# Linear attention of layer 1: from four passes of eight batches to one stream over eight groups of four batches

## The chip, the cores and the metric

The kernel runs on one core of one Trainium2 chip. Its engines work side by side: TensorE (matrix products, PE in the profile, its weight loads PEld), VectorE (DVE), ScalarE (ACT), GpSimd (POOL) and SyncE (SP, which here only issues transfers). Products land in PSUM, eight banks of 128 x 512 f32; everything else lives in SBUF. The metric is the device time of one execution in microseconds (us), the median of several.

## The reference, cut to what matters

The whole program is a decoder of four layers over x of 32 batches x 128 tokens x 128 channels. The change is in one sublayer, the attention of layer 1, followed by a residual sum and a layer norm:

```python
phi = lambda x: jax.nn.elu(x) + 1.0              # max(x, 0) + exp(min(x, 0))
q = phi(heads(x @ Wq.T + bq))                    # 16 heads of 8 channels
k = phi(heads(x @ Wk.T + bk))
v = heads(x @ Wv.T + bv)
kv = jnp.einsum('bhtd,bhtm->bhdm', k, v)
z = 1.0 / (jnp.einsum('bhtd,bhd->bht', q, k.sum(axis=2) + EPS) + EPS)
out = jnp.einsum('bhtd,bhdm,bht->bhtm', q, kv, z)
x = _layernorm(x + out.reshape(...) @ Wo.T + bo)
```

There is no mask in this sublayer, so each batch has one 128 x 128 summary k.T v, cut to the 16 diagonal blocks of 8 x 8 that belong to heads.

## The kernel before, in words

`decoder` runs the sublayers one after another. Each is a block of its own: every engine has its list of instructions, semaphores order them, and at the end of a block (`sublayer`, L31) all engines meet. `l1_attn` is called through `chunks("b", ...)` (L3092), which runs it four times, each time on eight batches (`NB = 8`, two groups of `GB = 4`) with buffers `r_b` and `xt_b`.

One pass, on eight batches:
- TensorE transposes the eight batches of x into two banks (L59), ScalarE copies them to `xt_b` (L1400). TensorE makes Q transposed for both groups (L1351, one product of 512 columns a group). Then, per group, K (L1356) with its bias as a second product of a row of ones with the bias row (L1358, weights of one row), four times, and V (L1356) four times.
- The feature map is elu + 1. VectorE takes from each bank the part below zero (L1427) and the part above (L1428), for Q with the bias as a per-partition number; ScalarE takes the exponential of the former (L1403), GpSimd adds the two (L1420). VectorE adds V's bias (L1432).
- Then a loop over the eight batches, one batch at a time, in three steps skewed by one batch each: summary (L1367, K features against V with a column of ones behind it, so that column 128 is the sum of K), mask (L1439, L1440, L1442), read-out (L1374, 144 columns: 128 of the result and 16 denominators), normalise (L1447, L1449, L1453), transpose (L1383), copy (L1407), output projection (L1386), residual (L1466).
- GpSimd has put x + bo into `r_b` beforehand (L1416). The layer norm takes statistics on VectorE (L68, L72), the root on ScalarE (L107), its reciprocal and the scaling on VectorE (L80, L83).

ScalarE needs one function table for the exponential and one for the root, and loads them in each pass (L102, L1403). f32 products are two records each in the trace, a high and a low half; transpositions are one record. The order of the work is the order in which the code is written; there is no planner.

Of the kernel before, what the change touches and what calls it, by code (L numbers as in the profile page):

```python
# [15 lines left out]
B_ALL = 32  # L16
# [1317 lines left out]
def l1_attn(nc, E):  # L1334
# [3 lines left out]
    with sublayer(nc, "xt_ps xt qk_ps v_ps neg pos ex q v kv_ps kvm ks kvd n_ps den rz zn zt_ps zt o_ps rb res" + LN) as (s, ctx):  # L1338
        sb = E.scratch(ctx)
        NEGP = sb("NEG", [P, 2 * NG, GT]); Q = sb("Q", [P, 2 * NG, GT])  # L1340
        V = sb("V", [P, NB, P + 1])
        KVD = sb("KVD", [P, 2, P + H]); KS = sb("KS", [P, NB]); DEN = sb("DEN", [P, 2, H]); RZ = sb("RZ", [P, 2, H])
        ZN = sb("ZN", [P, 2, P]); ZT = sb("ZT", [P, 2, P]); R = E.r
        with nc.Block() as block:
            @block.tensor
            def _(pe):
                for g in range(NG):
                    pe_transpose4(nc, [E.x[:, g * GB + b, :] for b in range(GB)], PS[:, g, :], E.ident).then_inc(s.xt_ps, 1)
                for g in range(NG):
                    pe.wait_ge(s.xt, g + 1)  # L1350
                    nc.tensor.matmul(PS[:, 2 + g, :], W.wq, E.xt[:, g * GT:(g + 1) * GT], start=True, stop=True).then_inc(s.qk_ps, 1)  # L1351
                for g in range(NG):
                    for w, b0, bank, sem in ((W.wk, W.bk, 4 + g, s.qk_ps), (W.wv, None, 6 + g, s.v_ps)):
                        for b in range(GB):
                            o = PS[:, bank, b * P:(b + 1) * P]
                            ins = nc.tensor.matmul(o, E.xt[:, (g * GB + b) * P:(g * GB + b + 1) * P], w, start=True, stop=b0 is None)  # L1356
                            if b0 is not None:
                                ins = nc.tensor.matmul(o, E.ones_row[0:1, :], b0, start=False, stop=True)  # L1358
                        ins.then_inc(sem, 1)

                def summary(t):
                    if t % GB == 0:
                        pe.wait_ge(s.q, NG + t // GB + 1)
                        pe.wait_ge(s.v, t // GB + 1)
                    if t >= 2:
                        pe.wait_ge(s.ks, t - 1)
                    nc.tensor.matmul(PS[:, t % 2, 0:P + 1], Q[:, NG + t // GB, (t % GB) * P:(t % GB + 1) * P], V[:, t, :],  # L1367
                                     start=True, stop=True).then_inc(s.kv_ps, 1)

                def read_out(t):  # L1370
                    pe.wait_ge(s.kvd, t + 1)
                    if t >= 2:
                        pe.wait_ge(s.zn, t - 1)
                    nc.tensor.matmul(PS[:, 2 + t % 2, 0:P + H], Q[:, t // GB, (t % GB) * P:(t % GB + 1) * P], KVD[:, t % 2, :],  # L1374
                                     start=True, stop=True).then_inc(s.n_ps, 1)

                def project(t):
                    pe.wait_ge(s.zn, t + 1)
                    if t >= 2:
                        pe.wait_ge(s.res, t - 1)  # L1380
                    else:
                        pe.wait_ge(s.q, 2 * NG)
                    nc.tensor.transpose(PS[:, 4 + t % 2, 0:P], ZN[:, t % 2, :], E.ident).then_inc(s.zt_ps, 1)  # L1383
                    pe.wait_ge(s.zt, t + 1)
                    o = PS[:, 4 + t % 2, P:2 * P]
                    nc.tensor.matmul(o, ZT[:, t % 2, :], W.wo, start=True, stop=True).then_inc(s.o_ps, 1)  # L1386

                for t in range(NB + 2):
                    if t < NB:
                        summary(t)  # L1390
                    if 1 <= t <= NB:
                        read_out(t - 1)
                    if t >= 2:
                        project(t - 2)

            @block.scalar
            def _(act):
                for g in range(NG):
                    act.wait_ge(s.xt_ps, g + 1)
                    nc.scalar.copy(E.xt[:, g * GT:(g + 1) * GT], PS[:, g, :]).then_inc(s.xt, 1)  # L1400
                for c in range(2 * NG):
                    act.wait_ge(s.neg, c + 1)
                    nc.scalar.activation(NEGP[:, c, :], NEGP[:, c, :], ACT.Exp).then_inc(s.ex, 1)  # L1403
                act_table(nc, E, ACT.Sqrt)
                for t in range(NB):
                    act.wait_ge(s.zt_ps, t + 1)
                    nc.scalar.copy(ZT[:, t % 2, :], PS[:, 4 + t % 2, 0:P]).then_inc(s.zt, 1)  # L1407
                    if t == GB:
                        act_layernorm(nc, act, E, s, 0)
                act_layernorm(nc, act, E, s, 1)  # L1410

            @block.gpsimd
            def _(pool):
                nc.gpsimd.memset(V[:, :, P:P + 1], 1.0)

                nc.gpsimd.tensor_tensor(R[:], E.x[:], bc(W.bo.unsqueeze(1), [P, NB, P]), ALU.add).then_inc(s.rb, 1)  # L1416
                for c in range(2 * NG):
                    pool.wait_ge(s.ex, c + 1)
                    pool.wait_ge(s.pos, c + 1)
                    nc.gpsimd.tensor_tensor(Q[:, c, :], Q[:, c, :], NEGP[:, c, :], ALU.add).then_inc(s.q, 1)  # L1420

            @block.vector
            def _(dve):
                for c in range(2 * NG):
                    dve.wait_ge(s.qk_ps, c + 1)
                    b = W.bq if c < NG else 0.0
                    nc.vector.tensor_scalar(NEGP[:, c, :], PS[:, 2 + c, :], b, 0.0, ALU.add, ALU.min).then_inc(s.neg, 1)  # L1427
                    nc.vector.tensor_scalar(Q[:, c, :], PS[:, 2 + c, :], b, 0.0, ALU.add, ALU.max).then_inc(s.pos, 1)  # L1428

                for g in range(NG):  # L1430
                    dve.wait_ge(s.v_ps, g + 1)
                    nc.vector.tensor_tensor(V[:, g * GB:(g + 1) * GB, 0:P], PS[:, 6 + g, :].rearrange("p (b d) -> p b d", b=GB),  # L1432
                                            bc(W.bv.unsqueeze(1), [P, GB, P]), ALU.add).then_inc(s.v, 1)

                def mask_summary(t):
                    dve.wait_ge(s.kv_ps, t + 1)
                    if t >= 2:
                        dve.wait_ge(s.n_ps, t - 1)
                    nc.vector.tensor_tensor(KVD[:, t % 2, 0:P], PS[:, t % 2, 0:P], E.blockmask, ALU.mult)  # L1439
                    nc.vector.tensor_scalar(KS[:, t:t + 1], PS[:, t % 2, P:P + 1], 1e-6, None, ALU.add).then_inc(s.ks, 1)  # L1440
                    dve.wait_ge(s.ks, t + 1)
                    nc.vector.tensor_scalar(KVD[:, t % 2, P:P + H], E.headmask, KS[:, t:t + 1], None, ALU.mult).then_inc(s.kvd, 1)  # L1442

                def normalise(t):
                    dve.wait_ge(s.n_ps, t + 1)
                    n = PS[:, 2 + t % 2, :]
                    nc.vector.tensor_scalar(DEN[:, t % 2, :], n[:, P:P + H], 1e-6, None, ALU.add).then_inc(s.den, 1)  # L1447
                    dve.wait_ge(s.den, t + 1)
                    nc.vector.reciprocal(RZ[:, t % 2, :], DEN[:, t % 2, :]).then_inc(s.rz, 1)  # L1449
                    dve.wait_ge(s.rz, t + 1)  # L1450
                    if t >= 2:
                        dve.wait_ge(s.zt_ps, t - 1)
                    nc.vector.tensor_tensor(ZN[:, t % 2, :].rearrange("p (h d) -> p h d", d=D), n[:, 0:P].rearrange("p (h d) -> p h d", d=D),  # L1453
                                            bc(RZ[:, t % 2, :].unsqueeze(2), [P, H, D]), ALU.mult).then_inc(s.zn, 1)

                for t in range(NB + 2):
                    if t < NB:
                        mask_summary(t)
                    if 1 <= t <= NB:
                        normalise(t - 1)  # L1460
                    if t >= 2:
                        u = t - 2
                        dve.wait_ge(s.o_ps, u + 1)
                        if u == 0:
                            dve.wait_ge(s.rb, 1)
                        nc.vector.tensor_tensor(R[:, u, :], PS[:, 4 + u % 2, P:2 * P], R[:, u, :], ALU.add).then_inc(s.res, 1)  # L1466
                    if t == GB + 1:
                        dve.wait_ge(s.res, GB)
                        dve_ln_stats(nc, dve, E, s, 0, grp(R, 0))
# [1757 lines left out]
```

## Time and profile before

| | us |
|---|---|
| median of 3 runs | 4504.68 (4503.95 to 4505.66) |
| the profiled execution, its own time | 4501.69 |
| span of the profiled execution | 4499.9 |
| TensorE busy | 3835.1 (85%) |
| VectorE busy | 2671.2 (59%) |
| ScalarE busy | 2146.1 (48%) |
| GpSimd busy | 1089.5 (24%) |

Busy shares are means over many stages with different limits; what is worth reading is the stage at hand, from 1474.56 us to 1635.62 us of the span. Times of the trace are given from the start of the span. A busy TensorE is not a TensorE at full speed: its clock is granted at 1.2 or 2.4 GHz, and the profile gives the granted share of full speed as PEclk (0.50 or 1.00 at any moment, a mean over a stretch).

### The profile page before, as it was taken

What the parts mean: (1) busy time and instruction counts of PE and PEld (TensorE: products, weight loads), DVE (VectorE), ACT (ScalarE), POOL (GpSimd) and SP (SyncE); (2) the same over time, 40 slices, a digit from 0 to 9 for tenths busy, and PEclk for the clock granted to TensorE, in tenths of its full rate; (3) what the DMA queues carried; (4) which work ended last, traced back from release to release, by engine and by line L of the source; (5) the groups of instructions that cost most, each with busy time, mean ns of one, the idle gap of its engine ahead of it and who ended that gap; (6) DMA issues with size and microseconds to landing.
All of it is one profiled execution on the core that took longest, in us unless ns stands there. A gap on an engine that the chain in (4) does not pass through costs nothing. (4 is left out here: it accounts for less than half of the span.)

```text
span 4499.9 us, 84989 instructions
## 1 busy us (share of the span) xinstructions
PE 3835.1 (85%) x33634; PEld 2573.7 (57%) x33634; DVE 2671.2 (59%) x7185; ACT 2146.1 (48%) x3795; POOL 1089.5 (24%) x754
## 2 busy tenths in 40 slices
PE   2888888787999789898999996555679998698999
PEld 2666666565666556664555553434457776465665
DVE  6677777565888557666656555982332222476555
ACT  2666666444555235555555444530554443454332
POOL 4444434222222211004454542221200000110000
PEclk8999999998999669999999997776789999798999
DMA  4222222000000010000000000004200000000000
GB/s 120 45 48 49 49 48 47 4 1 1 1 1 1 1 53 2 1 1 1 2 2 2 2 2 1 22 22 145 87 1 1 1 1 1 29 2 2 1 10 10
DMA packets 60472, 92.10 MB, mean 20 GB/s; under 512 B 16827, under 2 KB 43662, under 8 KB 58830
## 3 DMA queue, kind: packets, MB, share of 16 engines
q1 hardware_dynamic: 55948, 80.96, 7.7%
q8 instruction: 268, 4.39, 0.4%
q10 hardware_dynamic: 4130, 5.72, 0.4%
q14 instruction: 126, 1.03, 0.1%
HBM read 42.46 MB, written 10.62 MB: 12 GB/s over the span
## 5 line engine op out<-in xcount | busy, mean ns | idle before, releaser
L854 PE MATMUL banks<-XT,weight_region 128*128 128x512 f32 x1696 | 781.7, 599 | 1.4 <-DVE T L1229 1.4
L876 PEld LDWEIGHTS banks<-weight_region,HT 128*128 128x128 f32 x4672 | 560.8, 192 | 129.3 <-issue 107.4
L876 PE MATMUL banks<-weight_region,HT 128*128 128x128 f32 x4672 | 566.1, 275 | 7.1 <-ACT HT L1011 6.5
L1252 DVE SCALAR_TENSOR_TENSOR x_res<-banks,WT,x_res 128x128 f32<-128x128 f32 x800 | 225.0, 344 | 476.4 <-PE banks L876 437.4
L854 PEld LDWEIGHTS banks<-XT,weight_region 128*128 128x128 f32 x1696 | 305.8, 193 | 288.1 <-issue 285.3
L1006 ACT ACTIVATE HT<-banks,weight_region 128x512 f32<-128x512 f32 x256 | 173.3, 687 | 240.2 <-PE banks L854 234.0
L1069 POOL TENSOR_TENSOR FNM<-FNM,FRS 128x8 f32<-128x8 f32 x16 | 3.2, 202 | 1008.3 <-ACT FRS L965 1008.3
L458 DVE TENSOR_REDUCE MX<-banks 128x8 f32<-128x1152 f32 x128 | 173.2, 1353 | 116.6 <-PE banks L275 114.8
L384 ACT COPY PT<-banks 128x384 f32<-128x384 f32 x384 | 171.6, 481 | 134.1 <-PE banks L285 132.4
L1643 ACT COPY PT<-banks 77x512 f32<-77x512 f32 x256 | 143.0, 582 | 184.4 <-PE banks L1565 184.4
L1022 ACT ACTIVATE T<-banks 128x512 f32<-128x512 f32 x128 | 76.1, 597 | 233.9 <-PE banks L854 226.0
L285 PE MATMUL banks<-sb_c_ident,SM 128*128 128x128 f32 x1152 | 179.0, 283 | 4.6 <-ACT PT L384 2.7
L427 POOL TENSOR_TENSOR KT<-KT,FL 128x512 f32<-128x512 f32 x64 | 81.5, 1273 | 374.0 <-DVE FL L447 374.0
L258 PE MATMUL banks<-XT,weight_region 128*128 128x256 f32 x512 | 145.5, 414 | 28.4 <-ACT PT L384 24.6
L399 ACT ACTIVATE SM<-SM 128x1152 f32<-128x1152 f32 x128 | 150.3, 1174 | 29.6 <-DVE SM L466 29.6
L1565 PE MATMUL banks<-sb_c_ident,SM 128*77 128x128 f32 x1024 | 160.3, 291 | 0.0
L369 ACT ACTIVATE RAW<-banks,weight_region 128x256 f32<-128x256 f32 x256 | 107.3, 471 | 108.4 <-PE banks L258 99.6
L285 PEld LDWEIGHTS banks<-sb_c_ident,SM 128*128 128x128 f32 x1152 | 128.5, 141 | 47.2 <-ACT RAW L369 13.1
L466 DVE TENSOR_TENSOR SM<-banks,MX 128x1024 f32<-128x1024 f32 x128 | 155.3, 1213 | 0.0
L1081 POOL TENSOR_TENSOR x_res<-x_res,T 128x512 f32<-128x512 f32 x64 | 85.5, 1336 | 263.8 <-ACT T L983 263.8
L1214 DVE TENSOR_TENSOR HT<-banks,T 128x512 f32<-128x512 f32 x128 | 87.8, 690 | 100.6 <-PE banks L854 92.8
L1565 PEld LDWEIGHTS banks<-sb_c_ident,SM 128*77 128x77 f32 x1024 | 114.8, 151 | 53.2 <-issue 31.6
(488 smaller groups left out, 8529.7 us busy)
## 6 DMA issues: line engine op xcount, KB each, us to landing
FL<-RAW SPq DMA_DIRECT2D x512, 64.0 KB, 2.3
T<-s4d_k_dram SPq DMA_DIRECT2D x8, 1024.0 KB, 5.8
weight_region<-in_l_ffn__w_dram SPq DMA_DIRECT2D x2, 2048.0 KB, 7.6
film_dram<-F SPq DMA_DIRECT2D x8, 512.0 KB, 2.9
weight_region<-in_l_ffn__w_dram ACTq DMA_DIRECT2D x2, 2048.0 KB
FO<-film_dram SPq DMA_DIRECT2D x8, 512.0 KB, 4.1
x_res<-in_x_dram SPq DMA_DIRECT2D x1, 2048.0 KB
weight_region<-in_l_ffn__w_dram SPq DMA_DIRECT2D x2, 1024.0 KB, 9.7
```

What stands on the lines that cost most here:

```text
L258: ins = nc.tensor.matmul(bank[:, jj * PTOK:(jj + 1) * PTOK], w[:, j * P:(j + 1) * P], XT[:, p % 2, :], start=True, stop=True)
L285: ins = nc.tensor.transpose(ring(item, n)[:, q * P:(q + 1) * P], SM[:, n % 3, 3 * c + q, :], E.ident)
L384: nc.scalar.copy(PT[:, n % 2, 3 * c:3 * c + 3, :].rearrange("p h q -> p (h q)"), ring(f"T{c}", n)[:, 0:3 * P]).then_inc(s.pt, 1)
L399: nc.scalar.activation(SM[:, n % 3], SM[:, n % 3], ACT.Exp, scale=SCALE).then_inc(s.ex, 1)
L458: nc.vector.tensor_reduce(MX[:, n % 2], sc, AXX, ALU.max).then_inc(s.mx, 1)
L466: nc.vector.tensor_tensor(SM[:, n % 3, 1:9, :].rearrange("p (a i) k -> p i a k", a=2), sc[:, :, :, 0:P], bc(MX[:, n % 2].unsqueeze(3), [P, ...
L854: nc.tensor.matmul(PS[:, q % 4, :], w, xt, start=True, stop=True).then_inc(s.h_ps, 1)
L876: ins = nc.tensor.matmul(PS[:, 4 + u % 2, b * P:(b + 1) * P], HT[:, u % 2, j, b * P:(b + 1) * P], w2[j], start=j == 0, stop=j == len(w2) - 1)
L1006: ins = nc.scalar.activation(HT[:, u % 2, j, :], PS[:, (first[u] + j) % 4, :], ACT.Gelu, bias=W.b1[:, e, j:j + 1]).then_inc(s.act_done, 1)
L1252: ins = nc.vector.scalar_tensor_tensor(R[:, t, :], PS[:, 4 + u % 2, b * P:(b + 1) * P], WT[:, t, e:e + 1], R[:, t, :], ALU.mult, ALU.add)
L1565: ins = nc.tensor.transpose(bank_of("T", k)[0:L, c * P:(c + 1) * P], SM[:, t % 3, 4 * c + a, :], E.ident)
L1643: nc.scalar.copy(PT[:, t % 2, a].rearrange("p c q -> p (c q)"), bank_of("T", k)[0:L, :]).then_inc(s.pt, 1)
```

## The change

`l1_attn` is called once, on all 32 batches, as a loop over eight groups of four batches, software-pipelined: in step i TensorE turns group i+1, makes the summary of group i, turns back the result of group i-1, makes Q, K and V of group i+1, the output of group i-1 and the read-out of group i. Buffers of a group are two deep. The other parts:
- Work that was one batch to an instruction (mask, denominators, reciprocal, normalisation, copy of ZT, residual) now takes four batches, or two where a PSUM bank holds two (masks and ZN).
- Features: ScalarE takes relu(-x) from the bank (L1446, L1450 of the new code) and then exp(-that) (L1452, L1454); VectorE makes max(x, 0) + that in one instruction (L1468, L1472). GpSimd has no part in it.
- Biases of Q and of the output are made by products too, as K's was: Q's with the bias row as weights and ones as 512 columns (L1364), the output's with a row of ones as weights, per batch (L1400).
- The residual is added in x itself (L1510), without `r_b`. The layer norm's root and reciprocal are Ln and Exp on ScalarE (`act_rstd`), in the table that is loaded at the start.

```diff
-    with sublayer(nc, "xt_ps xt qk_ps v_ps neg pos ex q v kv_ps kvm ks kvd n_ps den rz zn zt_ps zt o_ps rb res" + LN) as (s, ctx):
+    NG = B_ALL // GB
...
+        XT = sb("XT", [P, 2, GT]); EQ = sb("EQ", [P, 2, GT]); EK = sb("EK", [P, 2, GT]); QF = sb("QF", [P, 2, GT]); KF = sb("KF", [P, 2, GT])
+        bank_xt, bank_q, bank_k, bank_v = PS[:, 0, :], PS[:, 1, :], PS[:, 2, :], PS[:, 3, :]
+        bank_o = PS[:, 5, :]
+        kv = PS[:, 4:6, 0:2 * KW].rearrange("p a (b k) -> p a b k", b=2)
+        nd = PS[:, 6:8, 0:2 * NW].rearrange("p a (b k) -> p a b k", b=2)
...
+                def project_in(g):
+                    x = XT[:, g % 2, :]
                     pe.wait_ge(s.xt, g + 1)
+                    if g:
+                        pe.wait_ge(s.qf, g)
+                    nc.tensor.matmul(bank_q, W.wq, x, start=True, stop=False)
+                    nc.tensor.matmul(bank_q, W.bq, bc(E.ones_row.unsqueeze(1), [1, GB, P]), start=False, stop=True).then_inc(s.q_ps, 1)
+                    if g:
+                        pe.wait_ge(s.kf, g)
+                    for b in range(GB):
+                        o = bank_k[:, b * P:(b + 1) * P]
+                        nc.tensor.matmul(o, x[:, b * P:(b + 1) * P], W.wk, start=True, stop=False)
+                        ins = nc.tensor.matmul(o, E.ones_row, W.bk, start=False, stop=True)
+                    ins.then_inc(s.k_ps, 1)
...
+                def turn_back(g):
+                    pe.wait_ge(s.zn, g + 1)
+                    pe.wait_ge(s.xt, min(g + 3, NG))
+                    pe_transpose4(nc, [ZN[:, g % 2, b, :] for b in range(GB)], bank_xt, E.ident).then_inc(s.zt_ps, 1)
+
+                def project_out(g):
+                    pe.wait_ge(s.zt, g + 1)
+                    pe.wait_ge(s.kvd, min(g + 2, NG))
+                    for b in range(GB):
+                        o = bank_o[:, b * P:(b + 1) * P]
+                        nc.tensor.matmul(o, ZT[:, g % 2, b, :], W.wo, start=True, stop=False)
+                        ins = nc.tensor.matmul(o, E.ones_row, W.bo[0:1, :], start=False, stop=True)
+                    ins.then_inc(s.o_ps, 1)
...
+                for i in range(-1, NG + 1):
+                    if i + 1 < NG:
+                        turn(i + 1)
+                    if 0 <= i < NG:
+                        summary(i)
+                    if 1 <= i:
+                        turn_back(i - 1)
+                    if i + 1 < NG:
+                        project_in(i + 1)
+                    if 1 <= i:
+                        project_out(i - 1)
+                    if 0 <= i < NG:
+                        read_out(i)
...
+                        nc.scalar.activation(EQ[:, g % 2, :], bank_q, ACT.Relu, scale=-1.0).then_inc(s.mq, 1)
...
+                        nc.scalar.activation(EQ[:, g % 2, :], EQ[:, g % 2, :], ACT.Exp, scale=-1.0).then_inc(s.eq, 1)
...
+                    if 2 <= i:
+                        act_rstd(nc, act, E, s, i - 2)
...
+                def features(g):
+                    dve.wait_ge(s.eq, g + 1)
+                    if g >= 2:
+                        dve.wait_ge(s.n_ps, g - 1)
+                    nc.vector.scalar_tensor_tensor(QF[:, g % 2, :], bank_q, 0.0, EQ[:, g % 2, :], ALU.max, ALU.add).then_inc(s.qf, 1)
...
+                for i in range(-1, NG + 2):
+                    if 0 <= i < NG:
+                        mask(i)
+                    if i + 1 < NG:
+                        features(i + 1)
+                        values(i + 1)
+                    if 1 <= i <= NG:
+                        residual(i - 1)
+                    if 0 <= i < NG:
+                        normalise(i)
+                    if 1 <= i <= NG:
+                        dve.wait_ge(s.res, i)
+                        dve_ln_stats(nc, dve, E, s, i - 1, grp(E.x, i - 1))
+                    if 2 <= i:
+                        dve_ln_scale(nc, dve, E, s, i - 2, grp(E.x, i - 2), grp(E.x, i - 2))
...
-        chunks("b", ("l1_attn", l1_attn, nothing))
+        run("l1_attn", l1_attn)
```

On TensorE, the loop over batches in a pass of the kernel before (L1367 summary, L1374 read-out, L1383 and L1386 transposition and output of the batch two before):

```order
L1367 MATMUL banks<-V,Q 128x129
L1374 MATMUL banks<-KVD,Q 128x144
L1383 MATMUL banks<-sb_c_ident,ZN 128x128
L1386 MATMUL banks<-weight_region,ZT 128x128
L1367 MATMUL banks<-V,Q 128x129
```

And TensorE through one whole group of the changed kernel, the read-out of one group first (L1409), then turn (L59 on x_res), summary (L1386), turn back (L59 on ZN), Q with bias (L1363, L1364), K (L1369, L1370), values (L1375) and the first batch of the output (L1399, L1400):

```order
L1409 MATMUL banks<-KVD,QF 128x144 x4
L59 MATMUL banks<-sb_c_ident,x_res 128x128 x4
L1386 MATMUL banks<-V,KF 128x129 x4
L59 MATMUL banks<-sb_c_ident,ZN 128x128 x4
L1363 MATMUL banks<-XT,weight_region 128x512
L1364 MATMUL banks<-sb_c_ones_row,weight_region 128x512
L1369 MATMUL banks<-weight_region,XT 128x128
L1370 MATMUL banks<-weight_region,sb_c_ones_row 128x128
```

The pair L1369, L1370 stands four times, then L1375 four times and the pair L1399, L1400 four times. Projections, which all stood ahead of the batch loop, now lie between the turn back of one group and the output of the same group.

On VectorE, the kernel before in the batch loop (mask of a batch, normalisation of the batch before, residual of the one before that):

```order
L1439 TENSOR_TENSOR KVD<-banks,sb_a_blockmask 128x128
L1440 TENSOR_SCALAR KS<-banks 128x1
L1442 TENSOR_SCALAR KVD<-sb_c_headmask,KS 128x16
L1447 TENSOR_SCALAR DEN<-banks 128x16
L1449 RECIPROCAL RZ<-DEN 128x16
L1453 TENSOR_TENSOR ZN<-banks,RZ 128x128
L1466 TENSOR_TENSOR r_b<-banks,r_b 128x128
```

And the changed one over a group of four batches, from the mask to the statistics:

```order
L1487 TENSOR_SCALAR KS<-banks 128x4
L1489 TENSOR_TENSOR KVD<-banks,sb_a_blockmask 128x2x128 x2
L1491 TENSOR_TENSOR KVD<-sb_c_headmask,KS 128x4x16
L1468 SCALAR_TENSOR_TENSOR QF<-banks,EQ 128x512
L1472 SCALAR_TENSOR_TENSOR KF<-banks,EK 128x512
L1480 TENSOR_TENSOR V<-banks,weight_region 128x4x128
L1510 TENSOR_TENSOR x_res<-banks,x_res 128x512
L1496 TENSOR_SCALAR DEN<-banks 128x64
L1498 RECIPROCAL RZ<-DEN 128x64
L1503 TENSOR_TENSOR ZN<-banks,RZ 128x256 x2
L68 BN_STATS ln_stats<-x_res 128x6 x4
```

Features, values and residual have moved between the mask and the normalisation, and seven instructions a batch have become ten a group ahead of the statistics.

## Rows read from the trace of the kernel before

**Rows 1.** Busy time by stretch: us, then each engine, PEclk, DMA share, GB/s
```profile
1453.00:1463.00 10.00, 10.00 (x46) 6.17 (x45) 7.97 (x12) 4.58 (x12) 2.54 (x2) 1.00 0.01 2
1474.56:1512.76 38.20, 29.66 (x116) 20.89 (x116) 22.77 (x92) 7.90 (x18) 7.11 (x6) 0.68 0.00 1
...
1593.90:1635.62 41.72, 34.22 (x116) 24.69 (x116) 23.32 (x92) 9.19 (x19) 7.09 (x6) 0.54 0.00 1
1474.56:1635.62 161.06, 128.94 (x464) 92.04 (x464) 92.26 (x368) 35.45 (x75) 28.50 (x24) 0.61 0.00 1
```

**Rows 2.** The same view, cut where the granted clock changes
```profile
1474.56:1480.48 5.92, 5.88 (x14) 3.42 (x14) 1.71 (x3) 1.80 (x3) 2.50 (x3) 0.50 0.01 3
1480.48:1483.89 3.41, 3.41 (x19) 2.55 (x19) 1.48 (x3) 0.63 (x1) 2.07 (x2) 1.00 0.00 0
1483.89:1494.13 10.24, 9.88 (x36) 7.53 (x34) 4.15 (x10) 2.75 (x4) 2.54 (x2) 0.50 0.00 0
1512.77:1518.02 5.25, 5.22 (x12) 3.08 (x13) 1.34 (x2) 3.01 (x4) 2.05 (x2) 0.50 0.00 0
...
1552.76:1558.98 6.22, 6.22 (x15) 3.71 (x16) 2.10 (x4) 3.08 (x4) 2.80 (x3) 0.50 0.00 0
...
1562.39:1582.87 20.48, 18.71 (x67) 14.46 (x66) 11.14 (x44) 3.81 (x8) 2.54 (x2) 0.50 0.00 0
...
1603.36:1634.73 31.37, 24.76 (x86) 18.58 (x84) 20.01 (x88) 5.47 (x14) 2.54 (x2) 0.50 0.00 1
```

**Rows 3.** Timeline of TensorE in pass 1: start, us, line, operation, records
```profile
1474.60 1.94 PE L59 MATMUL banks<-sb_c_ident,x_res 128*128 128x128 f32 x8 [7.87 <-PEq L48]
1476.36 3.79 PE L1351 MATMUL banks<-xt_b,weight_region 128*128 128x512 f32 x4
1479.93 0.64 PE L1356 MATMUL banks<-weight_region,xt_b 128*128 128x128 f32 x2
...
1480.91 0.49 PE L1356 MATMUL banks<-weight_region,xt_b 128*128 128x128 f32 x2
...
1481.74 0.49 PE L1356 MATMUL banks<-weight_region,xt_b 128*128 128x128 f32 x2
...
1486.15 0.80 PE L1356 MATMUL banks<-weight_region,xt_b 128*128 128x128 f32 x2
...
1487.59 0.80 PE L1356 MATMUL banks<-weight_region,xt_b 128*128 128x128 f32 x2
...
1490.49 2.08 PE L1356 MATMUL banks<-weight_region,xt_b 128*128 128x128 f32 x8
1492.63 1.20 PE L1367 MATMUL banks<-V,Q 128*128 128x129 f32 x4
```

**Rows 4.** Timeline of TensorE in the feed-forward stage before, granted clock 1.00
```profile
1461.18 1.45 PE L854 MATMUL banks<-XT,weight_region 128*128 128x512 f32 x3
1462.47 1.95 PE L876 MATMUL banks<-weight_region,HT 128*128 128x128 f32 x16
```

**Rows 5.** Groups of instructions, 1474 to 1636 us, and one of 1659 to 1661
```profile
L1439 DVE TENSOR_TENSOR KVD<-banks,sb_a_blockmask 128x128 f32<-128x128 f32 x32 | 9.0, 282 | 1.7 <-PE banks L1367 0.2
L1449 DVE RECIPROCAL RZ<-DEN 128x16 f32<-128x16 f32 x32 | 8.1, 253 | 1.1
L1432 DVE TENSOR_TENSOR V<-banks,weight_region 128x512 f32<-128x512 f32 x8 | 5.5, 687 | 0.5
...
L1714 DVE RECIPROCAL RZ<-banks 128x128 f32<-128x128 f32 x1 | 1.0, 958 | 0.4 <-PE banks L1580 0.4
```

**Rows 6.** Timeline of the stage's end
```profile
1631.74 0.87 DVE L68 BATCH_NORM_STATS2 ln_stats<-r_b 128x6 f32<-128x128 f32 x4
1632.65 0.38 DVE L72 BATCH_NORM_AGGREGATE ln_mv<-ln_stats 128x2 f32<-128x6 f32 x4
...
1633.61 1.12 DVE L83 TENSOR_SCALAR x_res<-r_b,ln_mv,ln_rstd 128x128 f32<-128x128 f32 x4
1635.62 0.33 SPq L1671 DMA_DIRECT2D weight_region<-in_l_attn__wq_dram  x1
```

## The prediction made before the changed kernel was run

> **What bounds the kernel now.** I read the page first: TensorE is busy 85% of the span and no other engine above 59%, but only one stage is edited, so the share that matters is that stage's. The busy time by stretch [rows 1] gives it: the linear attention of layer 1 runs from 1474.56 us to the first transposition of the next stage at 1635.62 us, 161.1 us in four passes of 38.2 to 41.7 us. TensorE is busy for 128.9 us of it (80%), VectorE 92.3, ScalarE 35.5, GpSimd 28.5. The reader is to see a second number in that row: the granted clock is 0.61. It has only the levels 0.50 (1.2 GHz) and 1.00 (2.4 GHz), so TensorE was at the upper one for 22% of the stage, whereas the feed-forward stage just before held 1.00 with TensorE fully busy. So the question is less how much idle time goes than how fast the products run.
>
> The same view cut at the changes of the clock [rows 2] shows when. Each pass starts at 1.2 GHz with eight transpositions and the products for Q; 5.92, 5.25 and 6.22 us later in the first three (the fourth is alike) the clock rises. Then come the products for K, each followed by a bias product with one row of weights, and 3.41 us after the rise the clock has fallen again, in all four passes within 0.01 us, though TensorE was busy for all 3.41 us. It stays low through the rest of the alternation with the bias (in passes 3 and 4 for 20.5 and 31.4 us). It rose once more 3.64 us after the values of pass 1 began, a run without bias products [rows 2, 3]. So a busy TensorE is not enough here: alternation with one-row products brings the clock down, solid runs bring it up.
>
> **The change part by part.** Sums are against the profiled execution (4501.69 us, span 4499.9); the median of the runs shown is 4504.68, 3.0 us more, and I add my difference to that.
>
> Removed: three of four pass starts and ends (barrier, fresh transpositions, drained pipeline), GpSimd's residual sum and feature sums, all ACT table switching inside the stage, and the batch-by-batch chain summary, mask, read-out, normalise, turn, project. Added on TensorE: per group one bias product for Q of 512 columns and four bias products for the output; before, 8 groups cost 464 records, now 8 x 68 = 544. VectorE loses its minimum and maximum passes and gets one fused pass for each of Q and K.
>
> TensorE per group, at 1.2 GHz [rows 3]: 4 transpositions 0.88 (eight took 1476.36 - 1474.60 = 1.76), twice, 1.76; Q product 1.79 (two took 3.57); its bias the same, 1.79, since 512 columns pass whatever the rows; K with bias 4 x 1.44 = 5.78 (1486.15 to 1487.59); values 2.14 (1490.49 to 1492.63); summary (129 columns) 2.16; output with bias as K, 5.78; read-out (144 columns) 2.41; changes of weights around Q's bias 0.3. Sum 23.9 us. At 2.4 GHz [rows 3, 4]: transpositions 2 x 0.49, Q and its bias 2 x 0.86 (three records of 512 columns took 1.29), K 4 x 0.83 = 3.34 (1480.91 to 1481.74), output 3.34, values 0.97 and summary 0.97 (sixteen records took 1.95), read-out 1.09, 0.2 for weights. Sum 12.6 us. Bounds of the two bias kinds that no row shows as such (512 columns with one row of weights; one-row bias after ZT): nothing if they hid under the neighbours, and the figures above if they pass at the rate of ordinary columns; the K rows show the latter, so I take it.
>
> VectorE per group [rows 5]: four passes of 128x512 at 0.69 (both features, values, residual) 2.75; two masks of 256 columns between 0.28 and 0.69 each, 0.45, and two ZN the same: 1.8; KS, head mask and DEN, small ones, at the 0.25 of the 16-column reciprocal, 0.75; reciprocal of 64 columns between 0.25 (16 columns) and 0.96 (128), 0.57; statistics and aggregates 1.3, scaling 1.1 [rows 6]. Sum 8.3 us, less than TensorE's at either clock. ScalarE: two copies and four activations at 0.60 (three took 1.80 in the first row of rows 2) and two small ones, about 4.2 us. So TensorE bounds the loop. Its waits: the turn back of group i-1 needs ZN, whose chain on VectorE after the read-out is 0.25 + 0.57 + 0.9 = 1.7 us; in front of it TensorE has turn and summary, 3.0 us at the low clock, so no wait, and 1.4 at the high one, so 0.3 to 0.4 us; behind that wait stand Q's product and all else of the group. The features of Q and K are waited for by the next summary only: after K is done, values, output and read-out (5.4 us at the high clock) cover relu, exponential and the fused pass, 2.0 us. GpSimd's and ScalarE's removed work was off the chain and counts nothing; if its cover were gone it would have been a gain of at most the 28.5 us of GpSimd [rows 1], and no wait on it stands between passes.
>
> Outside the groups: 0.9 us for the first XT copy, and after the last read-out 1.7 (ZN), 0.8 (ZT), then residual 0.7, statistics and aggregates 1.3, ScalarE's two 0.5, scaling 1.1, the end of the block 0.9 (1634.73 to 1635.62; [rows 6]) and some hand-overs, together 8.4 us. The instruction that starts the stage, a table load (1.2 us: four instructions with one took 3.01 in rows 2, three without 1.80), lies beside the first transpositions and their copy: 0.2 us.
>
> Hence the stage takes 8 T + 9, with T = 23.9 - 0.90 h where h is the time per group at 2.4 GHz (each us there does 23.9 / 12.6 = 1.90 us of low work). All low: 200 us. All high: 113 with the ZN waits. Everything hangs on h.
>
> What I take for h: a group has a solid run, read-out, turn, summary, turn back, Q, of 2.41 + 0.88 + 2.16 + 0.88 + 1.79 = 8.1 us at 1.2 GHz, and then 13.5 us of alternation broken only by the values. By rows 2 the rise comes 3.6 to 6.2 us into a solid run, so 1.9 to 4.5 us of it are left, 1.0 to 2.4 us at the upper clock; after that the clock outlives some 3.4 us of alternation, perhaps 1 to 2 us more where the values interrupt it. h is 4.4 to 7.8; I take 6.0. T = 18.5, the stage 148 + 9 = 157 us, 4 us less than 161.1. Forecast 4504.68 - 4 = 4501 us; with h from 4.4 to 7.8 the stage is 168.4 to 144.0, so its own range is 4488 to 4512.
>
> I weigh one rule of the Trainium skill here. Rows 2 show the clock falling while TensorE had no idle time. "TensorE: Matmul & The Clock Gate", Part 1, ties the drop to idle time of the engine and promises the full clock to sustained work. By that rule a loop in which TensorE hardly waits would stay at 2.4 GHz and the stage would be 113 us; the four falls in this trace speak against it.
>
> **The rivals.**
> A, the clock holds. Streaming without pass starts gives solid runs once a group, and the values lie between the two alternating stretches. If those keep the clock up for 10 us of a group, T is 14.9 and the stage 128 us: 4472. At all high it is 113, 4457. For it: TensorE is full as in the feed-forward stage at 1.00. Against it: all four alternations lost the clock. It is faster by more than the measurement can miss once h is above 6.7 (stage under 152).
> B, slower: the one-row products hold the clock down. Half of TensorE's low time is now alternation, the output's bias included, which before was a GpSimd addition. If a group gets only one rise of 3.4 us, T = 20.8, the stage 176 us: 4519. It decides from h below 4.2 (stage over 170). If the clock never rose, 200 us, 4544. For it: passes 3 and 4 had 20.5 and 31.4 us low in a row with TensorE 0.91 and 0.79 busy [rows 2]. Against it: the longest solid run there was shorter than 8.1 us, with waits in it.
> The same page of the Trainium skill, Part 4, says that transpositions do not count as activity; by that rule the two turns would cut the solid run into pieces and B would be what happens. The rise 5.25 us into a pass that began with 1.76 us of transpositions does not decide it.
> C, the loop does not stream: VectorE's queue, which has the mask ahead of the features and the normalisation behind the residual, makes TensorE wait each group. VectorE has 8.3 us in 18.5, so a wait would have to come from order, not load; each 1 us of it per group is 8 us, 4509. The order listing shows each wait with a group of other work ahead of it.
>
> **How the numbers follow.** A run-to-run spread of 1.7 us in the times and what moves in later stages make about 0.2%, 9 us, the least difference that I would call one. My forecast 0.50 (within 4496 to 4513), A 0.30, B 0.16, C 0.04. Faster 0.31, same 0.52, slower 0.17. The range for 8 in 10 goes to 4482 on A's side (h 8.6) and 4518 on B's.
>
> **What would show it.** In the new trace: TensorE over 95% busy in the stage, without a wait above 0.5 us per group but for the ends; the granted clock near 0.66 (h/T = 0.32), changing level once or twice in every group, up during the summary or Q product, down in K or output; a group of 128x512 each 18 to 19 us; K with bias at 0.83 or 1.44 us and nothing between; next stage's first transposition about 157 us after this stage's. It is wrong if the clock is 1.00 for several groups or 0.50 for several, or if VectorE ends the waits.

## The result, and the profile after

| | before | after |
|---|---|---|
| median, 15 runs each | 4504.74 us (4500.76 to 4507.90) | 4496.65 us (4493.07 to 4505.79) |
| the profiled execution, its own time | 4501.69 us | 4495.05 us |
| stage of the linear attention | 161.1 us | 150.6 us |

The ratio is 0.9984, 95% interval 0.9976 to 0.9992: 8 us, a small gain. The forecast was 4501 us, 4482 to 4518, "same" the likeliest.

The whole stage, four of its groups, and three stretches of one level of the clock, by busy time (columns as in the rows of before: us, PE, PEld, DVE, ACT, POOL, PEclk, DMA share, GB/s):

```profile
1474.84:1625.43 150.59, 138.72 (x544) 100.64 (x545) 57.14 (x192) 31.77 (x66) 0.15 (x2) 0.69 0.00 1
1525.00:1593.20 68.20, 68.20 (x274) 51.04 (x274) 28.54 (x96) 15.16 (x32) 0.00 (x0) 0.70 0.00 1
1491.34:1511.82 20.48, 19.48 (x100) 13.14 (x100) 7.13 (x19) 5.63 (x10) 0.00 (x0) 1.00 0.00 1
1532.30:1539.13 6.83, 6.83 (x34) 4.35 (x34) 3.10 (x17) 1.72 (x4) 0.00 (x0) 1.00 0.00 0
1539.13:1549.37 10.24, 10.24 (x38) 8.44 (x37) 4.12 (x9) 2.07 (x6) 0.00 (x0) 0.50 0.00 0
```

Against [rows 1] TensorE's records are 544 for 464 and its busy time 138.7 us for 128.9; VectorE is down from 92.3 to 57.1, GpSimd from 28.5 to nearly nothing (0.15). In the four groups TensorE has no idle time at all. From the fourth group on its clock is at the upper level for 6.8 us of a group and at the lower for 10.2, over and over; before that it was at the upper level for 20.5 us in one piece. The mean of the stage is 0.69 for 0.61. TensorE's timeline shows what it does at either level (start, us, line, operation, records):

```profile
1533.16 1.02 PE L1363 MATMUL banks<-XT,weight_region 128*128 128x512 f32 x2
1534.11 1.12 PE L1364 MATMUL banks<-sb_c_ones_row,weight_region 1*128 1x512 f32 x2
1535.16 0.49 PE L1369 MATMUL banks<-weight_region,XT 128*128 128x128 f32 x2
1535.58 0.48 PE L1370 MATMUL banks<-weight_region,sb_c_ones_row 1*128 1x128 f32 x2
...
1538.49 1.53 PE L1375 MATMUL banks<-weight_region,XT 128*128 128x128 f32 x8
1539.81 0.63 PE L1399 MATMUL banks<-weight_region,ZT 128*128 128x128 f32 x2
1540.37 0.79 PE L1400 MATMUL banks<-weight_region,sb_c_ones_row 1*128 1x128 f32 x2
...
1545.43 2.29 PE L1409 MATMUL banks<-KVD,QF 128*128 128x144 f32 x8
1547.51 1.06 PE L59 MATMUL banks<-sb_c_ident,x_res 128*128 128x128 f32 x4
1548.37 1.54 PE L1386 MATMUL banks<-V,KF 128*128 128x129 f32 x8
1549.74 0.60 PE L59 MATMUL banks<-sb_c_ident,ZN 128*128 128x128 f32 x4
1550.18 1.02 PE L1363 MATMUL banks<-XT,weight_region 128*128 128x512 f32 x2
```

From Q's product of one group to the next, 1533.16 to 1550.18, are 17.02 us. The clock falls at 1539.13, in the values, between K's alternation and the output's, and comes back at 1549.37, near the end of the summary, after a solid run of read-out, turn and summary. In the 20.5 us from 1491.34 the clock stood at 1.00 through K's alternation twice and the output's once, and fell at 1511.82, just behind them; an alternating stretch does not bring it down each time:

```profile
1493.96 0.48 PE L1370 MATMUL banks<-weight_region,sb_c_ones_row 1*128 1x128 f32 x2
...
1504.49 0.48 PE L1370 MATMUL banks<-weight_region,sb_c_ones_row 1*128 1x128 f32 x2
...
1508.71 0.48 PE L1400 MATMUL banks<-weight_region,sb_c_ones_row 1*128 1x128 f32 x2
...
1511.62 2.13 PE L1409 MATMUL banks<-KVD,QF 128*128 128x144 f32 x8
```

The alternation costs in itself as well: K with bias takes 3.33 us at 2.4 GHz (1535.16 to 1538.49) for twice the columns of the values, which take 0.97 us at that clock [rows 4]. The groups of VectorE that I had bounded:

```profile
L1468 DVE SCALAR_TENSOR_TENSOR QF<-banks,EQ 128x512 f32<-128x512 f32 x8 | 5.5, 692 | 49.3 <-ACT EQ L1452 49.3
L1489 DVE TENSOR_TENSOR KVD<-banks,sb_a_blockmask 128x256 f32<-128x256 f32 x16 | 6.0, 416 | 0.0
L1498 DVE RECIPROCAL RZ<-DEN 128x64 f32<-128x64 f32 x8 | 4.4, 554 | 0.3
```

0.69, 0.42 and 0.55 us for the 0.69, 0.45 and 0.57 assumed from [rows 5]. VectorE is waiting, not waited for. Its order listing stands for twelve instructions a group: nine in place of the seven of a batch, and three for features and values.

### The profile page after: what moved, and what is told of

Same layout as the page of the kernel before. It is cut to its first block and busy times, and to the rows that moved or that the text cites. A ratio compares the mean times of both kernels' runs of the same rounds, so it can differ in the third digit from the quotient of the medians.

```text
span 4493.0 us, 84833 instructions
## 1 busy us (share of the span) xinstructions
PE 3851.0 (86%) x33714; PEld 2584.7 (58%) x33714; DVE 2636.3 (59%) x7009; ACT 2140.7 (48%) x3785; POOL 1061.1 (24%) x731
```

## The experiments

Each was built on one of the two kernels and ran with the kernel before on the same chip (median 4506.3 us with the edits of block biases, 128 rows, one one-row product and four blocks with one row, 4505.1 with the others). "Stage" is from the stage's first transposition to the next stage's, in the profiled execution; each kernel has one, and its other executions are known by their time alone.

**The same columns, without alternation.** K's and the output's bias as one product of 512 columns each, ahead of the four products:

```diff
+                    nc.tensor.matmul(bank_k, E.ones_row, bc(W.bk.unsqueeze(1), [1, GB, P]), start=True, stop=False)
                     for b in range(GB):
-                        o = bank_k[:, b * P:(b + 1) * P]
-                        nc.tensor.matmul(o, x[:, b * P:(b + 1) * P], W.wk, start=True, stop=False)
-                        ins = nc.tensor.matmul(o, E.ones_row, W.bk, start=False, stop=True)
+                        ins = nc.tensor.matmul(bank_k[:, b * P:(b + 1) * P], x[:, b * P:(b + 1) * P], W.wk, start=False, stop=b == GB - 1)
...
```

> Changed kernel, but the biases of K and of the output come each as one product of 512 columns ahead of the four products of a group, where they were four products of 128 columns between them: the same columns with one row of weights, two changes of weight kind a group where there were sixteen. Theory 1 (the alternation costs time of its own and brings the clock down): TensorE per group at 2.4 GHz falls from 12.6 to 9.6 us, the clock stays at or near 1.00, a group takes about 10 us, the stage 150.6 -> about 91 us, the kernel about 4437 us. Theory 2 (a product costs its columns, and the clock follows the rest of the stage): stage 150 us, 4497 us.

Measured 4455.4 us, ratio 0.9888 (0.9871 to 0.9904); stage 106.9 us. Six groups in a row:

```profile
1503.00:1551.00 48.00, 46.19 (x275) 32.79 (x274) 32.24 (x104) 17.40 (x36) 0.00 (x0) 1.00 0.00 1
```

The clock is 1.00 and a group takes 10.23 us, as theory 1 had it. The stage is 16 us longer than its 91: its mean clock is 0.84, low for the first 16.4 us, for 3.4 us more soon after, and again in the drained end, where no projections lie between. Theory 2 is out.

**The same alternation, with 128 rows.** Every bias product gets weights of 1/128 in all rows against a replicated bias:

```diff
-                        ins = nc.tensor.matmul(o, E.ones_row, W.bk, start=False, stop=True)
+                        ins = nc.tensor.matmul(o, ONE[:], W.bk, start=False, stop=True)
...
```

> Changed kernel with the same products in the same order and of the same columns, but each bias product has 128 rows of weights of 1/128 against a replicated bias instead of one row. Theory 1 (it is the one row): the clock stays at 1.00, the pair of product and bias takes about 0.46 us instead of 0.83, TensorE 9.5 us a group, stage about 89 us, kernel about 4435 us, although TensorE multiplies more. Theory 2: nothing changes, 150 us and 4497 us. A third (accumulating into the same bank twice is what costs): clock and pair as now, 4497 us.

Measured 4445.9 us, 0.9869 (0.9854 to 0.9884); stage 96.2 us, groups of 9.52 us:

```profile
1475.50:1571.80 96.30, 80.28 (x544) 68.35 (x545) 56.59 (x192) 31.53 (x66) 0.11 (x3) 0.93 0.00 1
```

and TensorE's timeline at K with bias:

```profile
1516.76 0.38 PE L1372 MATMUL banks<-weight_region,XT 128*128 128x128 f32 x2
1516.98 0.39 PE L1373 MATMUL banks<-weight_region,ONE 128*128 128x128 f32 x2
1517.20 0.39 PE L1372 MATMUL banks<-weight_region,XT 128*128 128x128 f32 x2
```

The same 544 records in the same order. A pair takes 0.44 us instead of 0.83 and the mean clock of the stage is 0.93 instead of 0.69. The 7 us more than the 89 expected lie at the start and the end, since the groups take their 9.5. TensorE multiplies 128 times as much in its bias products, and the kernel is 51 us faster. So it is the single row: a change between 1 and 128 rows of weights costs 0.2 us at 2.4 GHz (0.39 us a pair, two changes), and without one-row products the clock holds. Theories 2 and 3 are out; the products accumulate here as they did before.

How the single row acts on the clock is less clear. Standing apart in wide products, as in the first edit, one-row products left the clock at 1.00 in the loop, with as many one-row columns as the changed kernel has. At the stage's start they went with a late rise: 16.4 us after the first transposition in that edit, as in the changed kernel (16.5), against 5.5 us with 128 rows:

```profile
1474.64:1491.06 16.42, 14.95 (x40) 8.80 (x40) 2.84 (x7) 4.65 (x7) 0.08 (x1) 0.50 0.00 1
1475.64:1481.15 5.51, 4.83 (x9) 2.37 (x10) 0.00 (x0) 1.56 (x2) 0.00 (x0) 0.50 0.01 1
```

Whether the clock goes by the rows themselves or by the time that passes at each change of weights is open: this edit took away both.

**One alternating stretch less.** The output's bias is added to x by GpSimd behind the transposition:

```diff
-                        ins = nc.tensor.matmul(o, E.ones_row, W.bo[0:1, :], start=False, stop=True)
...
+                for g in range(NG):
+                    pool.wait_ge(s.xt_ps, g + 1)
+                    nc.gpsimd.tensor_tensor(grp(E.x, g), grp(E.x, g), bc(W.bo.unsqueeze(1), [P, GB, P]), ALU.add).then_inc(s.rb, 1)
```

> Changed kernel, but the output's bias is added to x by GpSimd after the group's transposition; K keeps its four pairs and Q its bias product. Theory 1 (alternation costs its own time and the clock): TensorE 10.2 us a group at 2.4 GHz and 20.3 at 1.2, upper level for some 0.6 of the stage since one of the two alternating stretches is gone: 12.7 us a group, stage about 111 us, kernel about 4460 us. Theory 2 (columns only, a tenth of them gone): stage 137 us, 4483 us.

Measured 4472.3 us, 0.9932 (0.9913 to 0.9951), with runs from 4461 to 4475; stage 121.2 us, clock 0.75. Nearer to theory 1 (111 us) than to theory 2 (137), which is out by 16 us. Theory 1 is out by 10 us itself: with K's alternation alone the clock still goes down, and the upper share was 0.5, not the 0.6 I put in.

**One one-row product a group.** Also Q's bias off TensorE, K's as one product of 512 columns:

```diff
-                        nc.scalar.activation(EQ[:, g % 2, :], bank_q, ACT.Relu, scale=-1.0).then_inc(s.mq, 1)
+                        nc.scalar.activation(EQ[:, g % 2, :], bank_q, ACT.Relu, scale=-1.0, bias=BQ[:, 0:1]).then_inc(s.mq, 1)
...
-                    nc.vector.scalar_tensor_tensor(QF[:, g % 2, :], bank_q, 0.0, EQ[:, g % 2, :], ALU.max, ALU.add).then_inc(s.qf, 1)
+                    nc.vector.scalar_tensor_tensor(QF[:, g % 2, :], bank_q, BQ[:, 1:2], EQ[:, g % 2, :], ALU.add, ALU.max).then_inc(s.qf, 1)
```

> As the kernel with block biases for K, but the output's bias is added to x by GpSimd and Q's by constants of ScalarE and VectorE (max(x + b + 1, exp(min(x + b, 0)))), so that only one product with one row of weights is left per group. TensorE per group at 2.4 GHz about 7.8 us, VectorE 8.3 us. Theory 1: clock 1.00, VectorE now bounds the loop at about 9 us a group, stage about 81 us, kernel about 4427 us. Theory 2 (columns only): a fifth of TensorE's columns go, stage 122 us, 4468 us.

Measured 4437.8 us, 0.9854 (0.9839 to 0.9869); stage 90.7 us for 81 expected, groups of 8.95 us for 9; the difference is again the start at the low clock and the end. It is no longer TensorE's work that ends the group but a ring of waits (engine line waited for: us in total, times, longest us):

```profile
PE banks L1385 <- DVE x_res L1517: 4.5, 6, 1.1
PE banks L59 <- DVE ZN L1509: 3.7, 8, 1.7
```

The summary waits for the residual to free its bank, the turn back for ZN, which VectorE makes after it: 0.7 and 0.3 us of TensorE in a group. TensorE is idle for 1.1 us of a group and VectorE busy for 56.7 us of the stage, so that VectorE's queue seems to bound the loop by its order, not its load; no run with another order tests it.

**The passes back.** The changed kernel, and the one with 128 rows, as four blocks of two groups:

```diff
-        run("l1_attn", l1_attn)
+        for i in range(PASSES):
+            chunk(i)
+            run("l1_attn", l1_attn)
+        whole()
```

> Changed kernel as four blocks of two groups each, as the passes of the kernel before. If the gain of the change came from pass starts and ends, three more of them come back at 8.4 us and 0.9 us of block change each: stage about 178 us, kernel about 4524 us. If it came from instructions of four batches alone, the stage stays at 150 us and the kernel at 4497 us. In the mean clock the shares stay near 0.2 to 0.4 at the upper level.

> The kernel with full-row bias products, as four blocks of two groups. The three more starts and ends cost 9.3 us each if my sum of them holds (stage 96 -> 124 us, kernel 4474 us), and 14.6 us each if what the four blocks of one-row products cost was all waits and not clock (stage 140 us, 4490 us).

Measured 4539.2 us, 1.0074 (1.0059 to 1.0089), stage 194.4 us; and 4485.6 us, 0.9964 (0.9951 to 0.9977), stage 137.4 us. Three more starts and ends cost 43.8 us with one row and 41.2 us with 128, where the clock is 0.90: 14.6 and 13.7 us each, not the 9.3 of my sum. TensorE's busy and idle time tell the parts (stage of one row in four blocks first, 128 rows second):

```profile
1479.20:1673.60 194.40, 155.07 (x546) 105.28 (x545) 57.84 (x192) 35.94 (x69) 0.71 (x4) 0.63 0.00 0
1475.70:1613.10 137.40, 87.95 (x545) 68.78 (x546) 57.54 (x192) 35.22 (x69) 0.92 (x7) 0.90 0.00 1
```

With one row 27.5 of the 43.8 us are idle time of TensorE (39.3 for 11.9) and the rest is busy time at a lower clock (155.1 for 138.7). With 128 rows 33.4 of the 41.2 are idle time (49.4 for 16.0). What the sum left out shows in the waits of the latter:

```profile
PE banks L1388 <- DVE V L1483: 7.5, 4, 1.9
PE banks L1388 <- DVE KF L1475: 5.2, 4, 1.3
```

In a block of two groups each summary waits for the features or values just made, 12.7 us in four blocks; in the stream only the first two do, 2.8 us in all. That is 3.3 us for each further start, and with it the sum is 12.6.

**K's bias alone, in the kernel before.** The first edit, in the kernel before:

```diff
+                        if b0 is not None:
+                            nc.tensor.matmul(PS[:, bank, :], E.ones_row[0:1, :], bc(b0.unsqueeze(1), [1, GB, P]), start=True, stop=False)
...
-                            if b0 is not None:
-                                ins = nc.tensor.matmul(o, E.ones_row[0:1, :], b0, start=False, stop=True)
```

> The kernel before, with K's bias as one product of 512 columns ahead of the group's four products instead of four pairs. Theory 1: the first part of each pass loses 1.85 us per group at 1.2 GHz (1.5 at 2.4) and keeps the upper clock longer: stage 161 -> about 143 to 149 us, kernel about 4490 us. Theory 2 (columns only): 161 us, 4505 us.

Measured 4481.3 us, 0.9956 (0.9941 to 0.9971); stage 139.2 us:

```profile
1471.30:1610.50 139.20, 102.48 (x416) 70.92 (x416) 92.22 (x368) 35.43 (x75) 28.52 (x24) 0.68 0.00 1
```

Even more than theory 1 had (143 to 149), since the clock gains too: TensorE's busy time fell from 128.9 to 102.5 us and the mean clock rose from 0.61 to 0.68. One wide product in place of four narrow ones gives three times what the whole change gave (23.8 us for 8.1).

**The next stage.** Behind five of the kernels above (all but the four blocks with one row and the edit of the kernel before) the next stage, the cross attention, took 245 to 248 us from its first products to the next stage's, 8 to 13 more than the 236 and 237 of before and after. Its clock is low for up to 39 us from its start, but for one piece of 3.4 us. To test that, four products that nobody reads, at its first waits:

```diff
+                    for _ in range((2, 1, 1)[t] if t < 3 else 0):
+                        nc.tensor.matmul(PS[:, 7, :], E.ident, XT[:, 0, :], start=True, stop=True)
```

> As e3_no_pairs, with four products of 512 columns more at the start of each of the two cross attentions of this form, into a bank that is not in use yet, ahead of the scores of batches 0, 1 and 2, where TensorE waits for GpSimd and VectorE; their results are not read. If the 9 to 11 us that the next stage takes longer behind the faster linear attentions are its clock (at 1.2 GHz for 36 to 39 us from its start, against 19 in the kernel before), the clock rises within about 12 us, that stage returns to 236 us or less, kernel about 4427 us. If they are something else (loads of weights, queues), the four products only cost: up to 7 us each time, 4438 to 4452 us.

Measured 4429.3 us, 0.9842 (0.9824 to 0.9859), the fastest kernel of the study; against the 4437.8 of the same kernel without them, 8.6 us less for eight products more, four in each of the two cross attentions of this form. The first 39 us of the cross attention by busy time, without:

```profile
1568.40:1607.30 38.90, 32.73 (x228) 20.88 (x228) 14.16 (x12) 14.22 (x19) 10.91 (x9) 0.55 0.44 150
```

and with:

```profile
1565.60:1604.40 38.80, 34.10 (x386) 22.05 (x387) 22.36 (x22) 19.37 (x28) 12.05 (x10) 0.94 0.44 151
```

The clock is 0.94 for 0.55, TensorE gets through 386 records for 228, and that stage's first products to the next stage's are 235.4 us for 248.4. The clock had risen at 1569.89, 0.5 us before the first of the four products ran; without them it rose as early in the stage, and fell again after 3.4 us. So they kept it up and did not raise it.

How much of the 8.6 us this is stays open. The two profiled executions differ by 20 us: 13.0 in this stage and 6.6 in the cross attention of layer 3, which took 244.1 us without the four products, 237.5 with them, and 243.6 in the kernel before:

```profile
3839.76:4083.89 244.13, 213.52 (x3037) 149.64 (x3037) 161.94 (x285) 127.74 (x209) 29.71 (x21) 0.92 0.04 15
3826.61:4064.14 237.53, 208.84 (x3045) 146.28 (x3045) 161.84 (x285) 127.43 (x209) 29.68 (x21) 0.96 0.04 15
3894.37:4137.98 243.61, 213.44 (x3038) 149.60 (x3037) 161.90 (x285) 127.75 (x209) 29.68 (x21) 0.92 0.04 15
```

There the four products gain 6 us though nothing had been given back. The kernel without them ran at 4435 to 4440 us in three executions and at 4447 in the profiled one, so the 248.4 us may be an unlucky start of the clock in that one. The kernel before with the four products was not run.

## Why the prediction was right, and where its steps were off

- What bounds the stage: TensorE, by its clock. Right; from the fourth group on it has no idle time in the loop, and the two edits that only touch how biases are multiplied move the stage by 44 and 54 us.
- The stage as 8 T + 9: 150.6 us measured for 157, from two errors that work against each other. The clock was at the upper level for 58 us of the stage (20.5 us once, 6.8 five times, 3.4 once), 7.3 us a group. With this h the sum gives T = 17.4 and 139 us for the groups, and TensorE was busy for 138.7, 9 us less than my 148. Beside that it was idle for 11.9 us where I had 9. What I had summed came out (0.8 at the start, 1.7, 0.7 and 4.9 at the end); what no term had were 2.4 us at the end, in which the output waited for the last mask (1601.1 to 1603.5), and 1.4 in the first groups.
- h, the term on which everything hung: 7.3 us in the mean and 6.8 in the last groups where I took 6.0, within its 4.4 to 7.8. It came about much as put: the rise lay 3.9 us into the solid run (1545.43 to 1549.37), 1.8 us of it were left at the upper clock, and then the clock outlived 5.1 us of Q's bias, K's alternation and the first values, where I had 3.4 and 1 to 2 more. Two early groups were shorter, 10.5 and 14.1 us, with the clock up for 20.5 us in a row; the forecast had no such stretch, and that the mean stayed within its bounds is in part luck.
- The sum of a group at the low clock was a little high: 17.02 us with 6.83 of them at 2.4 GHz make 23.2 us of low work for my 23.9, the read-out 2.08 us for 2.41 above all.
- The clock once up and once down in every group: right from the fourth group on. The return came in the summary, as put; the fall came in the values, between the two alternations, and not in K's or the output's. TensorE was busy for 92% of the stage where I had put over 95.
- One-row products cost their columns at the neighbours' rate plus changes of weights: right for 512 columns (Q with its bias took 2.00 us, 1533.16 to 1535.16, for my 1.72 and 0.2) and for those behind ZT (four pairs took 5.62 us, 1539.81 to 1545.43, for my 5.78).
- ZN's wait: none at the low clock, 0.33 us at the high one, as put. K's features, which I had covered by other work, were waited for once, for 0.67 us, in an early group at the high clock.
- Starts and ends: 9.3 us was too small for the old cut, 13.7 to 14.6 us. Only one is left in the forecast, but it sets the account of the change. In four blocks the new work takes 194 us, 33 more than before, and the stream takes 44 away again. The one-row products are what makes the four blocks slow: with 128 rows they take 137.4 us, 24 less than before. In the stream they cost 54 us (150.6 for 96.2), most of what the change could have gained over the 161.1 of before.
- Rival A (the clock holds): wrong for this kernel, right in the loop once the alternation with single rows is gone. The Trainium skill's rule ("TensorE: Matmul & The Clock Gate", Part 1), by which a TensorE without idle gaps stays warm, is not what this trace shows: 10.2 us of each group are at 0.50 with TensorE busy for all of it, as far as the profile tells busy time. Rival B (one rise of 3.4 us a group): wrong. That transpositions would not count for the clock (the Trainium skill, the same page, Part 4) no run here isolates; they stand in the solid run in which the clock rises. B, which the prediction drew from it, did not happen with eight of them in each group. Rival C: wrong here; the kernel with one one-row product has such waits.
- The kernel gained 8.1 us in the median, 6.6 in the profiled executions, of which the stage is 10.5. The 3.8 us that came back lie behind it, 1.0 in the cross attention (236.8 for 235.8 us) and 3.1 in one stage of layer 2 (241.4 for 238.3 us); what they are was not traced. The forecast had the stage at 4 us less and nothing elsewhere, so that the kernel came nearer to it, 4496.7 for 4501, than the stage did; that part is luck.

## What to carry to other kernels

In this kernel a bias by a product was cheap only where it had the rows of its neighbours, or stood apart in one wide product: interleaved one-row products cost 0.2 us at every change at 2.4 GHz, and the clock was lower with them (0.69 for 0.93 over the stage). Read PEclk beside busy time: a TensorE at 100% may be at half speed, and then an edit that adds multiplications can be the faster one. And follow the clock into the next stages: it can start low there, as it did for most of 39 us here.

## What the runs showed of the hardware that was not expected

The granted clock does not follow busy time. With the same 544 records, TensorE busy for nearly all of the loop, it was 0.69 in the mean with one-row and 0.93 with 128-row bias products. It fell into step with the program: four groups of 17.02 us in a row, each 6.8 us up and 10.2 down, after 20.5 us at the upper level with the same products. With wide one-row products at the stage's start it rose 16.4 us after the first transposition, without them 5.5 us after it, in one profiled execution each. And the start of the cross attention was at the low level for most of 39 us (0.55) with TensorE busy for 32.7 of them, or at the high one (0.94) with four products more.
